# Gated attention and expert layer: weight pieces spread anew over the batches, and turned rows copied ahead of the statistics

## The reference

```python
# attention, per batch; ctx is 512 x 128
Q, K = ctx @ Wq.T, ctx @ Wk.T
sim = Q @ K.T / (sqrt(32) * 4)
threshold = the 153rd largest value of each row of sim
A = sigmoid(sim) * (sim >= threshold)
A = (A + A.T) / 2
x = x + tanh(g_xattn) * ((1 - gamma) * layernorm(x) + gamma * A)
# feed-forward, on all 2048 rows
h = layernorm(x)
y, g = split(h @ shared_gw.T)              # 704 columns each
shared = (silu(g) * y) @ shared_dw.T
s = sigmoid(h @ gate_w.T)                  # 8 experts
top 2 of s + gate_bias; their s, divided by their sum, are the weights
out = shared + sum of the 2 experts' (silu(h @ Wg.T) * (h @ Wu.T)) @ Wd.T times weight
x = x + tanh(g_ffn) * out
```

## Time and profile before

| | us |
|---|---|
| median of 3 runs (586.65 to 587.45) | 587.41 |
| profiled execution | 586.68 |
| its span, first to last instruction | 584.8 |
| busy: PE 504.6, DVE 339.8, ACT 256.3, POOL 214.9 | |

### The profile page before, as it was taken

One profiled execution on the slowest core, in us unless ns is written; L12 is line 12 of the kernel. 1 busy time (PEld: TensorE's weight loads), 2 busy tenths in 40 slices (PEclk: granted clock), 3 DMA queues, 4 the chain that ended last, 5 costly groups with the idle time before them and its releaser, 6 DMA issues.

```text
span 584.8 us, 10606 instructions
## 1 busy us (share of the span) xinstructions
PE 504.6 (86%) x3141; PEld 281.4 (48%) x3142; DVE 339.8 (58%) x719; ACT 256.3 (44%) x468; POOL 214.9 (37%) x229
## 2 busy tenths in 40 slices
PE   2456399598998899879877999999999999999992
PEld 0134244244444444434354566666666666666660
DVE  0698469767788778868995576433333333333330
ACT  1492756728674866554451265332222222223221
POOL 2201324830267116812543034434433433443422
PEclk9866679898999999989999999999999999999997
DMA  4411141323225222440225689554444454454433
GB/s 143 159 46 48 31 141 38 113 77 123 77 76 151 109 91 58 117 154 21 84 58 166 198 234 245 86 97 73 78 97 76 76 87 88 72 88 91 72 49 42
DMA packets 28597, 57.50 MB, mean 98 GB/s; under 512 B 3664, under 2 KB 3920, under 8 KB 28560
## 3 DMA queue, kind: packets, MB, share of 16 engines
q1 hardware_dynamic: 19824, 36.60, 19.9%
q0 software_dynamic: 8736, 20.45, 19.6%
HBM read 37.90 MB, written 19.14 MB: 98 GB/s over the span
## 4 chain that ended last, share of the span: by engine, by line
PE 54%; DVE 22%; ACT 10%; issue 6%; DMA 4%; POOL 2%; SPq 0%; DVEq 0%; POOLq 0%; ACTq 0%
PE py L1063 13%; PE pg L1043 12%; PE pu L1044 12%; PE pt_bank L839 3%; DVE w L1168 3%; PE pa L1053 2%; DVE work L1318 2%; ACT w L596 2%; PE py L926 2%; DVE w L1260 2%; PE pg L903 2%; DVE pa L1198 2%; PE pu L903 2%; DMA stage<-in_weights 1%; DVE w L1202 1%
## 5 line engine op out<-in xcount | busy, mean ns | idle before, releaser
L1043 PE MATMUL pg<-w,x_t 128*128 x468 | 140.8, 313 | 0.0
L1044 PE MATMUL pu<-w,x_t 128*128 x468 | 140.7, 313 | 0.0
L557 POOL DMA_INDIRECT out<-rows,idx x39 | 61.8, 1585 | 142.2 <-ACT rows L779 129.2
L1063 PE MATMUL py<-w,work 128*128 x351 | 82.1, 379 | 0.7 <-DVE work L1525 0.7
L903 PE MATMUL pg<-w 128*128 128x512 f16 x288 | 79.1, 392 | 3.6 <-DVE work L1318 3.6
L769 ACT ACTIVATE work<-pg 128x352 f32<-128x352 f32 x39 | 18.0, 462 | 129.9 <-PE pu L1044 129.9
L903 PE MATMUL pu<-w 128*128 128x512 f16 x240 | 67.6, 392 | 0.0
L596 ACT ACTIVATE w<-stage 128x544 f16<-128x544 f32 x80 | 50.8, 648 | 27.5 <-DMA stage<-in_weights 24.2
L502 POOL TENSOR_TENSOR w<-stage,w 128x544 f16<-128x544 f32 x42 | 55.3, 1332 | 11.5 <-DVE w L1285 10.0
L516 POOL TENSOR_TENSOR work<-work 128x512 f16<-128x512 f32 x20 | 24.1, 1205 | 95.4 <-ACT work L678 94.5
L1514 DVE SCALAR_TENSOR_TENSOR work<-pu,work 128x352 f32<-128x352 f32 x39 | 20.4, 524 | 64.4 <-ACT work L769 64.4
(11 more groups left out here) (222 smaller groups left out, 777.3 us busy)
## 6 DMA issues: line engine op xcount, KB each, us to landing
stage<-in_weights SPq DMA_DIRECT2D x80, 272.0 KB
w<-in_x SPq DMA_DIRECT2D x4, 1024.0 KB, 6.4
xn_rows<-w SPq DMA_DIRECT2D x16, 256.0 KB, 2.0
out<-w SPq DMA_DIRECT2D x16, 256.0 KB, 2.1
w<-in_ctx_t SPq DMA_DIRECT2D x4, 256.0 KB, 3.1
out<-rows,idx POOLq DMA_INDIRECT x39, 4.7
work<-xn_rows,idx POOLq DMA_INDIRECT x20
xg<-xn_rows,idx POOLq DMA_INDIRECT x19
```

The lines of the kernel that those rows point to most:

```text
L557: pool.indirect_dma_start(out=out, out_offset=bass.IndirectOffsetOnAxis(ap=idx[:, t:t + 1], axis=0), in_=rows[:, t % 2, :], in_offset=None ...
L1043: pe.matmul(pg[p][:, 0:H], lhs, w[:, item, half, at:at + H], start=begin, stop=end)
L1044: mm = pe.matmul(pu[p][:, 0:H], lhs, w[:, item, half, at + H:at + 2 * H], start=begin, stop=end)
L1063: mm = pe.matmul(py[:, :], hid_t[:, p, part * JC + j, :], w[:, item, half, at:at + C], start=(j, part, half) == (0, 0, 0), stop=(j, part) ...
```

## The change

It changes where the 48 early pieces are made. `FIRST` becomes 8. The slots become one row per round: 14, 13 and 13 pieces, none in the last batch, and behind the last unit of the three rounds stand 4, 8 and 8. For units 1 to 3 ACT's and POOL's pieces go ahead of the unit's high and low half instead of behind it. Batch 0's first down product waits unit by unit for the pieces that it reads. At the start ACT's pieces 6 and 7 go ahead of the copies of the second projection, PE makes the low halves of pieces 4 and 5 earlier, and batch 0's order is its own: rows turned as soon as they can be, ahead of the tanh and of the statistics. In the later seams DVE copies the first turned tile and adds tile 2 ahead of the next scores' statistics. In the last batch ACT makes a unit's silu ahead of the high half of the unit before, and DVE's pieces of item 6 stand otherwise between the row additions.

```diff
@@ -20,10 +20,8 @@
 SLOTS_STEP = 4
 SLOTS_STEPS = TOPK * TILES // SLOTS_STEP
 BY_PE = 6
-FIRST = 10
-SLOT_PIECES = (0, 1, 2, 2, 2, 3)
-PER_PERIOD = sum(SLOT_PIECES)
-LAST_PIECES = (2, 2, 2, 2, 0, 0)
+FIRST = 8
+SLOT_PIECES = ((2, 2, 2, 2, 2, 4), (0, 1, 2, 2, 0, 8), (0, 1, 2, 2, 0, 8))
 KEEP = int(SEQ * 0.3)
 UP_W = KC * 2 * H
 ITEM_W = UP_W + JC * C
@@ -275,16 +273,12 @@
         def low_uses(k):
             return [j for j in range(k) if low_pair(j) == low_pair(k)]
 
-        def period_pieces(b):
-            k = FIRST + b * PER_PERIOD
-            slots = []
-            for count in SLOT_PIECES if b < BATCHES - 1 else LAST_PIECES:
-                slots.append([(j // CHUNKS, j % CHUNKS) for j in range(k, k + count)])
-                k += count
-            return slots
-
         def pieces_by(b, u):
-            return FIRST + b * PER_PERIOD + sum((SLOT_PIECES if b < BATCHES - 1 else LAST_PIECES)[:u])
+            return FIRST + sum(sum(slots) for slots in SLOT_PIECES[:b]) + sum(SLOT_PIECES[b][:u]) if b < len(SLOT_PIECES) else LATE * CHUNKS
+
+        def slot_pieces(b, u):
+            begin = pieces_by(b, u)
+            return [(k // CHUNKS, k % CHUNKS) for k in range(begin, begin + SLOT_PIECES[b][u])]
 
         def late_pieces(t):
             begin = LATE_FIRST + t * PER_TILE
@@ -382,7 +376,7 @@
 
             def next_pieces(b, slots):
                 for u in slots:
-                    for item, n in period_pieces(b)[u]:
+                    for item, n in slot_pieces(b, u):
                         k = item * CHUNKS + n + RING
                         if k < LATE * CHUNKS:
                             load_piece(k // CHUNKS, k % CHUNKS)
@@ -405,7 +399,6 @@
             for b in range(BATCHES - 1):
                 together(b, b + 2 < BATCHES)
             store_shared(BATCHES - 2, TPB - 1)
-            next_pieces(BATCHES - 1, range(UPS))
 
             load_item(LATE)
             store_shared(BATCHES - 1, 0)
@@ -526,13 +519,17 @@
             o.clear()
 
             def together(b, more):
-                slots = period_pieces(b)
                 for u in range(UPS):
                     if u == TPB - 1:
                         base_scalars(b + 1)
-                    shared_low(b, u)
-                    for piece in slots[u]:
-                        low_piece(*piece)
+                    if 0 < u < TPB:
+                        for piece in slot_pieces(b, u):
+                            low_piece(*piece)
+                        shared_low(b, u)
+                    else:
+                        shared_low(b, u)
+                        for piece in slot_pieces(b, u):
+                            low_piece(*piece)
                 row_scalars(b + 1, 0)
                 row_scalars(b + 1, 1)
                 if more:
@@ -543,8 +540,6 @@
                 together(b, b + 2 < BATCHES)
             for u in range(UPS):
                 shared_low(BATCHES - 1, u)
-                for piece in period_pieces(BATCHES - 1)[u]:
-                    low_piece(*piece)
 
 
             def gather(t):
@@ -682,6 +677,12 @@
                     keep_qk(b + 1)
                 for i in range(TPB):
                     normalised(b, i)
+                if b == 0:
+                    rows_turned(b, 1)
+                    keep_scores(b + 1)
+                    rows_turned(b, 3)
+                    score_tanh(b + 1)
+                    return
                 if more:
                     keep_scores(b + 1)
                     score_tanh(b + 1)
@@ -706,17 +707,14 @@
             high_piece(0, 4)
             low_from_banks(3)
             high_piece(0, 5)
+            low_from_banks(4)
             high_piece(0, 6)
+            low_from_banks(5)
+            high_piece(0, 7)
             keep_qk(1)
-            low_from_banks(4)
-            high_piece(0, 7)
-            low_from_banks(5)
-            for k in range(CHUNKS, FIRST):
-                high_piece(k // CHUNKS, k % CHUNKS)
             scores_and_rows(0, True)
 
             def together(b, more):
-                slots = period_pieces(b)
                 count(b + 1, 0)
                 keep_logits(b)
                 count(b + 1, 1)
@@ -727,11 +725,15 @@
                     if u in (1, 2):
                         scaled_sigmoid(b + 1, 2 * u - 2)
                         scaled_sigmoid(b + 1, 2 * u - 1)
+                    if 0 < u < TPB:
+                        for piece in slot_pieces(b, u):
+                            high_piece(*piece)
                     shared_high(b, u)
                     if u == 0:
                         count(b + 1, 3)
-                    for piece in slots[u]:
-                        high_piece(*piece)
+                    if u == 0 or u >= TPB:
+                        for piece in slot_pieces(b, u):
+                            high_piece(*piece)
                 scores_and_rows(b + 1, more)
 
             for b in range(BATCHES - 1):
@@ -749,9 +751,9 @@
             router_exp()
             for u in range(UPS):
                 shared_silu(BATCHES - 1, u)
-                shared_high(BATCHES - 1, u)
-                for piece in period_pieces(BATCHES - 1)[u]:
-                    high_piece(*piece)
+                if u:
+                    shared_high(BATCHES - 1, u - 1)
+            shared_high(BATCHES - 1, UPS - 1)
             for s in sh_st:
                 after(act, s, (BATCHES - 1) * (TPB // 2) * 16)
             for n in range(CHUNKS):
@@ -907,8 +909,6 @@
 
             def shared_down(b, i, pieces=range(UPS)):
                 bank_ = down_bank(b, i)
-                if b == 0 and 0 in pieces and i == 0:
-                    pieces_ready(HALVES * CHUNKS)
                 if 0 in pieces:
                     after(pe, y_sb, b * TPB + max(0, i - 1))
                     if bank_ is pu[0]:
@@ -918,6 +918,8 @@
                     after(pe, hlo_sb, b * UPS + u + 1)
                     cols = slice(i * P, (i + 1) * P)
                     half, at = shared_down_at(u)
+                    if b == 0 and i == 0:
+                        pieces_ready(half * CHUNKS - (-(at + C) // CHUNK_W))
                     if u == MIXED:
                         pe.matmul(bank_[:, :], hid_tb[:, u, 0, cols], w[:, half, 0, at:at + C], start=False, stop=False)
                         mm = pe.matmul(bank_[:, :], hid_tb[REST:, u, 0, cols], w[REST:, half, 1, at:at + C], start=False, stop=True)
@@ -932,15 +934,14 @@
             for i in range(TPB):
                 scores(0, i)
             pe.wait_ge(const_ok, 2)
-            low_pieces(0, RING)
+            low_pieces(0, RING + 1)
             missed_rows(0)
+            low_pieces(RING + 1, BY_PE)
             after(pe, w_lo[RING - 1], 1)
             turn_attention(0)
             project(1, None)
-            low_pieces(RING, RING + 1)
             for i in range(TPB):
                 scores(1, i)
-            low_pieces(RING + 1, BY_PE)
             for i in range(TPB):
                 turn_batch(0, i)
             pe.wait_ge(gw_ok, 1)
@@ -1284,22 +1285,25 @@
                         o.wait(made)
                     dve.tensor_tensor(xnr[:, i, C:2 * C], xn[:, i % 2, :], xnr[:, i, 0:C], ALU.subtract).then_inc(xn_lo, 1)
 
-                for i in (0, 2):
-                    if i and b == 0:
-                        after(dve, xn_lo, b * TPB + i)
-                    made = [exact(i), exact(i + 1)] if b == 0 else [None, None]
-                    low_rows(i, made[0])
-                    low_rows(i + 1, made[1])
-                after(dve, up_mm, b * UPS)
-                if shared is None:
+                if b == 0:
+                    made = [exact(0), exact(1)]
+                    low_rows(0, made[0])
+                    low_rows(1, made[1])
+                    after(dve, xn_lo, TPB // 2)
+                    made = [exact(2), exact(3)]
                     rows_turned(b, 0)
+                    low_rows(2, made[0])
+                    low_rows(3, made[1])
                     rows_turned(b, 2)
                     score_stats(b + 1, range(TPB))
                 else:
+                    for i in range(TPB):
+                        low_rows(i, None)
+                    shared_rows(shared, 2)
+                    after(dve, up_mm, b * UPS)
+                    rows_turned(b, 0)
                     if more:
                         score_stats(b + 1, range(TPB))
-                    shared_rows(shared, 2)
-                    rows_turned(b, 0)
                     rows_turned(b, 2)
                     if not more:
                         shared_rows(shared, 3)
@@ -1503,9 +1507,9 @@
             for n in range(RING):
                 low_piece(LATE, n)
             shared_rows(BATCHES - 1, 0)
-            for n in range(RING, CHUNKS):
+            shared_rows(BATCHES - 1, 1)
+            for n in range(RING, CHUNKS - 2):
                 low_piece(LATE, n)
-            shared_rows(BATCHES - 1, 1)
 
 
             def hidden(t, p):
@@ -1532,6 +1536,8 @@
 
```

(2 more changed lines are left out.)

## The result

The changed kernel takes 573.23 us (median of 4 runs, 572.74 to 574.20) against 587.03 of the kernel before in the same comparison: ratio 0.977 [0.975, 0.979], 13.8 us less. It is faster, but the forecast of 563.2 us (557 to 571) is missed by 10.0 us. The profiled execution took 572.87 us with a span of 571.1, at a mean granted clock of 0.942.

A forecast was written before the change was run, and what follows sets the result against it. The prediction took whichever wait ends last, ahead of the expert stage, to bound the kernel. Its terms, 9.0 + 3.8 + 1.2 + 1.6 + 6.3 + 2.3 = 24.2 us, gave 563.2 us, range 557 to 571.

The forecast's parts named there:

- Term 1: Start: FIRST 10 to 8 and new orders bring batch 0's first up matmul 9.0 us earlier, bounds 7 to 10.
- rival of another wait at the start: Start: the earlier rows meet a wait the trace does not show, half of the 9.0 goes; 567.7, chance 0.08.
- Term 2: Batch 0: 14 pieces and a down product waiting unit by unit add 3.8 us of gain, bounds 2 to 6.
- Term 3: Batches 1 and 2: slots 0, 1, 2, 2, 0, 8 bring hidden 5 2.4 us earlier, 0.6 left each, 1.2 together.
- POOL's eight pieces take over 13 us: Batches 1 and 2, behind the last unit: a stated sign that would show the forecast wrong.
- the clock stays up: Rival, seams between batches: less idle time keeps PE's clock up, 1.3 to 1.9 us at each of two; 560.0, chance 0.15.
- rival of the eight pieces ending later: Batches 1 and 2, last unit: loads land late, POOL ends at 190.7, not 187.5, 3.2 us each; 569.6, chance 0.2.
- The copy ahead of the statistics: Seams into batches 1 and 2: DVE's turned-row copy ahead of score_stats gains 0.8 us each, 1.6 together, bounds 0.4 to 2.
- Term 4: Last batch: without its eight pieces, which hold DVE on POOL, 6.3 us gained, 5 to 7 in other cases.
- Term 5: Hand-over to the experts: shared_rows(1) ahead of DVE's low pieces 6 and 7 of item 6 gains 2.3 us, bounds 1 to 3.

The follow-up runs named there:

- e4: The kernel before with the new start alone: FIRST = 8, freed two pieces behind batch 0's unit 0, new PE, ACT and DVE orders; 575.36 us, 0.981.
- e3: The changed kernel with four instead of eight pieces behind the last unit of batches 1 and 2, and eight again in the last batch; 572.13 us, 0.974.
- e6: The changed kernel with the hand-over undone: DVE's four later pieces of item 6 back in one block ahead of shared_rows 1; 576.57 us, 0.986.
- e9: The changed kernel with DVE's order in the seams behind batches 0 and 1 undone: statistics ahead of tile 2 and first turned copy; 572.68 us, 0.978.
- e11: The changed kernel with ACT's order in the last batch undone: a unit's high half directly behind its silu; 572.21 us, 0.977.
- e1: The changed kernel with unit 3's two pieces behind that unit's halves again in batches 1 and 2, on ACT and POOL; 569.41 us, 0.970.
- e2: The changed kernel with POOL's base_scalars behind unit 3's low half and pieces instead of ahead of them; 570.46 us, 0.973.
- e7: The changed kernel with e2's edit and slots (1, 2, 2, 2, 0, 6) in batches 1 and 2; 561.86 us, 0.960.
- e8: The changed kernel with e2's edit, six pieces behind batch 0's last unit, slots (1, 2, 2, 2, 0, 5) in batches 1 and 2; 563.07 us, 0.962.
- e10: e7 with unit 3's pieces behind its halves instead of ahead in batches 1 and 2; 567.02 us, 0.967.
- e5: The kernel before with only batch 0's first down product waiting unit by unit for the pieces it reads; 579.99 us, 0.992.

## Why the prediction was wrong

**Term 1, start, 9.0: right.** 9.3 measured, and e4 shows all of it from this part alone. ACT's first rows start at 55.98 instead of 65.24, the first up at 64.92. The rival of another wait at the start did not come.

**Term 2, batch 0, 3.8 and 0.8 at its seam: 3.1 measured.** The mechanism is right: the 6.0 us wait is gone, two short ones of 1.17 and 0.30 us stand in its place, and the attention is turned 42.1 us after the first up (forecast 41.9). DVE's row addition starts 44.5 us after it (109.38) instead of 43.7, and the seam gave 0.24 us instead of 0.8. The sum had slipped too: by its own times the row addition moves from 47.0 us behind the first up (122.57 - 75.55) to 43.7, which is 3.3 us and not 3.8. L1199 (L1198 of before) beside POOL's piece and low half costs 1.4 us: a pair took 2.65 us where pairs alone take 1.30, within the bounds of 0 to 2.4. A silu waits for low 3 here too, and DVE's hidden 5 waits 2.90 us behind it.

**Term 3, batches 1 and 2, 1.2: the step that failed.** It had two faults of its own, and the clock came on top. The first: "The two pieces of slot 4 leave from between silu 4 and silu 5, so hidden 5 ... comes at 173.9." The same sum noted that low 3 still follows `base_scalars` and its pieces, and charged that to PE alone. But the silu of unit 5 needs the same low half. This second waiter took back 2.0 of the 2.4 us; the clock took 0.8 more in batch 1 (2.9 in all), 1.0 in batch 2. The silu waited 3.30 or 3.31 us for low 3 in batches 1 and 2 of all five profiles that keep `base_scalars` and two pieces ahead of it (after, e3, e6, e9, e11), and under 0.1 us in all five that do not (e1, e2, e7, e8, e10). e1 and e2, which take the work ahead of it away in two ways, bring hidden 5 forward by 1.5 to 2.8 us.

How much of such a difference is clock can be read off. Before and after differ in the granted clock of the first 8 us behind the first up, within which the lower level ended in every batch of the table (before, then after; batches 1 and 2 each):

```profile
142.59:150.59 8.00, 8.00 (x37) 3.36 (x35) 5.52 (x21) 4.02 (x13) 0.00 (x0) 0.83 0.39 119
203.12:211.12 8.00, 8.00 (x36) 3.32 (x34) 5.54 (x21) 3.70 (x11) 0.00 (x0) 0.79 0.33 123
...
128.87:136.87 8.00, 8.00 (x33) 3.19 (x31) 5.45 (x21) 3.19 (x10) 0.00 (x0) 0.72 0.35 133
192.79:200.79 8.00, 8.00 (x31) 3.09 (x28) 5.76 (x23) 2.74 (x9) 0.00 (x0) 0.66 0.37 119
```

A clock of 0.83 there means that about 2.7 us ran at the lower level and the rest at the full one. If PE sets the pace, half of that time is lost, which is 8 us x (1 - clock). Taken off the measured part, it leaves this (batch 1, batch 2):

| kernel | clock of the first 8 us | up to hidden 5 | the same less the clock's loss |
|---|---|---|---|
| before | 0.83, 0.79 | 33.72, 34.06 | 32.3, 32.4 |
| e4 | 1.00, 1.00 | 32.38, 32.38 | 32.4, 32.4 |
| e5 | 1.00, 0.81 | 32.38, 33.88 | 32.4, 32.3 |
| after | 0.72, 0.66 | 34.19, 34.64 | 32.0, 32.0 |
| e9 | 0.78, 0.79 | 33.74, 33.70 | 32.0, 32.0 |
| e1 | 0.68, 0.78 | 32.74, 32.00 | 30.2, 30.2 |
| e2 | 0.77, 0.79 | 31.94, 31.85 | 30.1, 30.1 |
| e7 | 0.78, 1.00 | 32.86, 31.15 | 31.1, 31.1 |
| e10 | 0.78, 1.00 | 33.28, 31.54 | 31.5, 31.5 |

The last column is the same in both batches of a kernel and in kernels with the same code there, which is what bears the estimate out. So the move of slot 4's pieces brought hidden 5 forward by 0.4 us where 2.4 were forecast, and without the wait for low 3 it would have been 2.1 to 2.2 (e1, e2): the price was right, the second waiter was missing.

The second fault is "ends at 176.7 + 8 x 1.35 = 187.5". Counted from hidden 5, POOL was to begin 2.8 us and to end 13.6 us after it; it began 4.0 and ended 15.6 after it. The 4.0 us are the same in e2 and e7, where low 3 is early. The price of a piece was 11.56 / 8 = 1.44 us: five at 1.38, then three at 1.22 with 0.28 to 0.38 us of hand-over ahead of each, behind ACT and its loads. That is 0.8 us; the later beginning is 1.2, and 0.2 was spare. Since eight pieces were by my own sum within 0.6 us of the old time, every microsecond missed went straight to the end. "POOL's eight pieces take over 13 us" was the wrong test: at 11.56 they were already too long.

Together, batch 1: 2.9 us at hidden 5, 1.8 behind it and 0.2 at the seam, 4.8 in all (rounded). Batch 2 lost 5.6 in the same way, and 1.1 of that in its seam: PE stood idle 6.30 us ahead of the turn, and the nine matmuls behind it ran at half level. Before had an idle time of 3.59 us at the same place, and its nine matmuls ran at that level only in part (after, then before):

```profile
247.00 1.01 PE L841 MATMUL pt_bank<-ident,w 128*128 128x128 f16 x8 [6.30 <-DVE w L1286]
247.81 4.04 PE L928 MATMUL py<-w,work 128*128 128x512 f16 x9
...
253.44 0.61 PE L839 MATMUL pt_bank<-ident,w 128*128 128x128 f16 x8 [3.59 <-DVE w L1285]
253.88 3.36 PE L926 MATMUL py<-w,work 128*128 128x512 f16 x9
```

In batch 1's last units nine such matmuls took 2.12 us. PE was busy at the lower level for 5.8 us of this seam in after and for 3.4 in before; half the difference, 1.2 us, is an estimate of what the clock cost here, and the seam became 1.1 us longer. The granted clock of batch 2 was 0.88 where before had 0.94: the rival "the clock stays up" went the other way. In all, of the 8.4 us by which batches 1 and 2 became longer, about 3.0 are clock (0.8 and 1.0 up to hidden 5, 1.2 in the last seam). The forecast had no term for it, and its rival had the other sign. The rival of the eight pieces ending later (569.6) had the right place, and loads landing late as its mechanism; ACT did wait for loads there, 1.69 us once and under 0.3 after, but most of the loss was not theirs.

**The copy ahead of the statistics, 0.8 a seam:** 0.24 and 0.62 by comparison with before, 1.05 and 1.45 undone from after (e9), none of it told apart in the total.

**Term 4, 6.3: right** (6.6, e3 and e11: all from the pieces). **Term 5, 2.3:** 2.9 against before, 4.8 undone from after (e6). The lower clock behind a wait was not in the term; in the profile of before there was none at this place to be lost. The expert stage, +1.1, is not the change's: in thirteen profiled executions it took 258.8 to 260.7 us with the same instructions.

The balance of 24.2: 1.5 less in batch 0, 10.4 less in batches 1 and 2, 1.1 less in the experts; 0.3 more at the start, 0.9 in the last batch, and 1.4 ahead of the first piece by the chance of the execution: 13.8.

Batch 1 of the kernel before took 33.72 us up to hidden 5 in its own profile and 32.38 in e4 and e5, which have its code there unchanged. By the table that is the clock alone. So a difference of 1.3 us in that part of one batch decides nothing before the clock is taken out; the 15.7 us from hidden 5 to `row_scalars` needs no such care, it came in both batches of all six profiles with eight pieces (15.65 to 17.00). Left open: why the lower level lasted longer behind the seams of the changed kernel. PE stood 2.23 us for ACT's turned copy (L656) in both seams there, and 1.3 to 2.0 us in before; nothing here isolates that.

## What to carry to other kernels

When work leaves one engine's queue, list everyone who waits for each item of the queue that is left full: a late item that one waiter could bear may be the next thing for another. Work moved behind the last unit of a stage is free only up to the moment when the next instruction's input is there (here 12.1 us behind hidden 5, five to six pieces), so fill it to that moment counted from the measured start, and put the rest where there is room: once `base_scalars` was out of the way, six behind and one more in each of two early slots took 8 us off what eight behind took by the ratios (e7 against e2; 4.0 by their profiled executions, of which e2's was its fastest and e7's its slowest). Before two profiles are compared stage by stage, take the clock's part out: it moved the same code by up to 1.7 us a batch here. And a gain in one stage is to be weighed against its price in the others: eight pieces out of the last batch gained 6.6 us and cost 6.6 in two others.

## What the runs showed of the hardware

- After an idle time PE's next matmuls can run at the lower level: behind 6.30 us of waiting nine matmuls took 4.04 us (2.12 otherwise); behind 3.00 us in e6 twelve took 4.45 (2.75 otherwise), but behind 2.41 us in the kernel before 2.77. The length of the idle time alone does not order the cases: behind 2.53 us in e5 twelve took 4.45, behind 3.31 us in e4 2.76. Such a wait can cost over one and a half times its length.
- Where PE sets the pace, a stretch at the lower level costs half its length: 8 us x (1 - granted clock) explains the parts up to hidden 5 of batches 1 and 2 to within 0.1 us in the nine kernels of the table, between clocks of 0.66 and 1.00.
- DVE and POOL hold each other up in single instructions: one of the eight L1471 took 1.28 us instead of 0.31 where it met a low half on POOL, and two L1199 took 2.65 instead of 1.30 beside a piece and a low half. The Trainium skill's page "SBUF — State Buffer", section "Who interferes with whom", says that a VectorE instruction with two SBUF inputs, which both are, and a GpSimd instruction that reads SBUF shut each other out for a whole instruction. These rows agree with it in kind. Of the 1.8 us by which eight pieces exceeded 8 x 1.22, 0.8 lies in the first five, which run beside DVE's L1261 and its row additions, and 1.0 is hand-over between ACT and POOL.
